# A program that ends with a 256-token tile, the last hidden part split first in front of 128-token tiles, and results handed on by block

## The chip, the cores and the metric

The kernel runs on one core of one Trainium2 chip. The metric is the device time of one execution in microseconds. TensorE (PE) multiplies, ScalarE (ACT) and VectorE (DVE) work element by element, GpSimd (POOL) issues the indirect DMAs, SyncE (SP) issues the others. Every engine works off its own queue in order and waits on semaphores.

## What is computed

Two stages follow each other: an attention of 4 x 1024 tokens over 77 context rows, added to x, and then a mixture of experts, cut here to its core:

```python
logits = jnp.einsum('bsh,he->bse', x, Wr)              # 9 experts, the best two are taken
topk_w, topk_idx = jax.lax.top_k(jax.nn.softmax(logits, axis=-1), 2)
gate = jax.nn.silu(jnp.einsum('th,ehi->tei', xf, Wg))  # 256 -> 704
hidden = gate * jnp.einsum('th,ehi->tei', xf, Wu)      # 256 -> 704
out = jnp.einsum('tei,eih,te->th', hidden, Wd, cw)     # 704 -> 256, weighted by the gate
```

The change touches only the second stage.

## The kernel before

The attention writes each token's row twice, once into the region of each of its two experts, in a DRAM table `expert_in`. The expert stage then works through 40 tiles, t = 0 to 39, listed in `TILES` (L93 to L98). A **pair** tile has two blocks of 128 tokens, a **single** tile one block. There are 3 early pairs, 29 further pairs, numbered 0 to 28, and 8 singles; `SINGLES_AFTER` (L74) names the pairs behind which a single stands. In the kernel before, the last single stands behind pair 28 and is tile 39, the last of all.

All matrices are kept as a rounded part (`hi`) and a rest (`lo`), and each product is three matmuls (`product`, L338). One tile goes through this:

- **gate and up products** (PE, `gate_up`, L1354): a pair has three units, u = 0, 1, 2, of 24, 24 and 18 matmuls of 256 columns. A single has 18 wider matmuls in one go (`single_gate_up`).
- **silu** of the gate half (ACT, `silu`), times the up half (DVE, `hidden`, gives `hid_f`), rounded by ACT (`hid_round`, gives `hid_hi`), rest by DVE (`hid_rest`, gives `hid_lo`). I call this the hidden chain; the last unit's is the "last inner part". A single's product is turned by six transposes on PE (`hid_turn`, L1448) before it is rounded.
- **down product** (PE, `down`, L1458): 34 matmuls of 256 columns for a pair (17 for each block), 17 for a single.
- **result**: ACT scales it by the gate weight (`res_move`, L1155, one ACTIVATE for each block), POOL adds it to the output in DRAM by an indirect DMA for each block (`add_results`, L927), and waits for their landing before it copies the next tile's token numbers (`note`).

While tile t is in work, the weights of tile t + 1 are split in six pieces, two at each unit of a pair: ACT rounds them (`round_pieces`, L1099, gives `wgt_hi`), DVE makes the rests (`rest_pieces`, L1932, gives `wgt_lo`). The first four pieces are the gate and up weights, which `gate_up(t + 1, 0)` waits for; the last two (1280 and 256 columns) are the down weights.

The order is written by hand. PE does the down product of a tile in the next tile's step: for a pair behind u = 1, for a single behind its gate and up products (`pair_step`, `single_step`, L1481 to L1495). At each unit of a pair step, ACT runs silu, two weight pieces, `hid_round`; DVE runs `hidden`, two rests of weights, `hid_rest`. In a single step, DVE runs the single's product, two rests, the rests of the turned tokens (`tok_rest`), two more rests, and then the single's hidden rests.

Of the kernel before, what the change touches and what calls it, by code (L numbers as in the profile page):

```python
# [70 lines left out]
EARLY_SEEN = 27  # L71
NP = 2 * B * S // W - EARLY
NS = 8
SINGLES_AFTER = (2, 6, 10, 13, 17, 21, 24, 28)  # L74
SEGS = 2 * E
assert EARLY_SEEN * 2 * P >= E * EARLY_ROWS
SPARE = 5 * W
# [27 lines left out]
def is_pair(t):  # L105
    return TILES[t][0] > 1
# [11 lines left out]
def program(nc, x, ctx_rows, fside, ln1_w, ln1_b, ln2_w, ln2_b, wq, wkv, wout, wr, wg, wu, wd, out):  # L118
# [3 lines left out]
    with ExitStack() as ctx:  # L122
# [210 lines left out]
        def turned_hid(t):  # L333

            return (unit_banks(t, 1)[:, 1, :].rearrange("p (c n) -> p c n", n=P), bank[5 - t % 2][:, KT * P:KT * P + P],
                    bank[5 - t % 2][0:FHALF, KT * P + P:KT * P + 2 * P])

        def product(to, a, b, first, last):  # L338

# [420 lines left out]
        def _(pool):  # L760
# [166 lines left out]
            def add_results(t):  # L927

                i = t % 2
                pool.wait_ge(res_ready, t + 1)  # L930
                for a in range(TILES[t][0]):
                    nc.gpsimd.indirect_dma_start(out, bass.IndirectOffsetOnAxis(ap=tok_id[i][:, a:a + 1], axis=0),  # L932
                                                 res[i][:, a, :], None, compute_op=ALU.add).then_inc(added, 16)
                pool.wait_ge(added, BLOCKS_TO[t + 1] * 16)
# [14 lines left out]
        def _(act):  # L949
# [172 lines left out]
            def silu(t, u):  # L1122

                q = (UNITS_TO[t] + u) % 2
                act.wait_ge(gu_done, UNITS_TO[t] + u + 1)
                if u < UNITS - 1:
                    nc.scalar.activation(gate_act[q][:], unit_banks(t, u)[:, :, 0:W], ACT.Silu).then_inc(silu_done, 1)
                else:
                    nc.scalar.activation(gate_act[q][:, 0, :], unit_banks(t, u)[:, 0, 0:W], ACT.Silu)
                    nc.scalar.activation(gate_act[q][FHALF:P, 1, :], unit_banks(t, u)[0:FHALF, 1, 0:W], ACT.Silu).then_inc(silu_done, 1)  # L1130
# [23 lines left out]

            def res_move(t):  # L1155
                i = t % 2
                act.wait_ge(down_done, t + 1)
                act.wait_ge(tok_noted, t + 1)
                if t > 1:
                    act.wait_ge(added, BLOCKS_TO[t - 1] * 16)  # L1160
                for a in range(TILES[t][0]):
                    ins = nc.scalar.activation(res[i][:, a, :], bank[6 + i][:, a * D:(a + 1) * D], ACT.Copy, scale=tok_gate[i][:, a:a + 1])  # L1162
                ins.then_inc(res_ready, 1)

            def pair_step(t):

                ahead = EARLY - 1 <= t < NT - 1
                src = weights_of(t + 1) if ahead else None
                for u in range(UNITS):
                    silu(t, u)  # L1170
                    if ahead:
                        round_pieces(t + 1, u, src)
                    hid_round(t, u)
                    if u == UNITS - 2 and t:
                        tok_move(t + 1)
                        if t == 2:
                            act.wait_ge(last_stored, 16)
                        res_move(t - 1)
# [30 lines left out]
        def _(pe):  # L1209
# [248 lines left out]
            def down(t):  # L1458

                i, blocks = t % 2, TILES[t][0]  # L1460
                pe.wait_ge(*down_split(t))
                pe.wait_ge(hid_ready, UNITS_TO[t + 1])
                if t > 1:
                    pe.wait_ge(res_ready, t - 1)
                elif t:
                    pe.wait_ge(tail_row_made, 1)
                    pe.wait_ge(slot_ready, T)
                else:
                    pe.wait_ge(att_added, T)
                w = [down_of(x[half_of(t)]) for x in (wgt_hi, wgt_lo)]  # L1470
                for a in range(blocks):
                    to = bank[6 + i][:, a * D:(a + 1) * D]
                    h = [x[:, :, a * P:(a + 1) * P] for x in hid[i]]
                    for f in range(FC - 1):
                        product(to, [x[:, f, :] for x in h], [x[:, f, :] for x in w], f == 0, False)

                    for x in w:
                        mm = nc.tensor.matmul(to, h[0][:, FC - 1, :], x[:, FC - 1, :], start=False, stop=x is w[1])  # L1478
                mm.then_inc(down_done, 1)

            def pair_step(t):  # L1481

                for u in range(0 if t else UNITS - 1, UNITS):
                    gate_up(t, u)
                    if u == UNITS - 2:
                        tok_turn(t + 1)
                        down(t - 1)

            def single_step(t):
# [15 lines left out]
        def _(dve):  # L1505
# [483 lines left out]
            def pair_step(t):  # L1989

                src = weights_of(t + 1) if t < NT - 1 else None
                for u in range(UNITS):
                    hidden(t, u)
                    if t < NT - 1:
                        rest_pieces(t + 1, u, src)
                    hid_rest(t, u)
                    if t < NT - 1 and u == UNITS - 2:
                        tok_rest(t + 1)

# [68 lines left out]
```

## Time and profile before

| | us |
|---|---|
| median of 3 runs | 855.67 (854.84 to 857.24) |
| the profiled execution | 854.76 |
| its span, from the first to the last instruction | 853.1 |
| PE busy | 805.5 (94% of the span) |
| DVE busy | 669.4 (78%) |
| ACT busy | 620.8 (73%) |
| POOL busy | 368.2 (43%) |
| share of PE in the chain that ended last | 84% |

The expert stage takes about the second half of the span. Rows of the timeline give, in this order: start in us, duration in us, engine, line, operation, what is written and read, and how many are merged. A bracket at the end gives the engine's idle time just before, and what ended it.

### The profile page before, as it was taken

What the parts mean: (1) busy time and instruction counts of PE and PEld (TensorE: products, weight loads), DVE (VectorE), ACT (ScalarE), POOL (GpSimd) and SP (SyncE); (2) the same over time, 40 slices, a digit from 0 to 9 for tenths busy, and PEclk for the clock granted to TensorE, in tenths of its full rate; (3) what the DMA queues carried; (4) which work ended last, traced back from release to release, by engine and by line L of the source; (5) the groups of instructions that cost most, each with busy time, mean ns of one, the idle gap of its engine ahead of it and who ended that gap; (6) DMA issues with size and microseconds to landing.
All of it is one profiled execution on the core that took longest, in us unless ns stands there. A gap on an engine that the chain in (4) does not pass through costs nothing.

```text
span 853.1 us, 19506 instructions
## 1 busy us (share of the span) xinstructions
PE 805.5 (94%) x6007; PEld 761.1 (89%) x6007; DVE 669.4 (78%) x1624; ACT 620.8 (73%) x1959; POOL 368.2 (43%) x534
## 2 busy tenths in 40 slices
PE   5999999999999999789699999999999999999993
PEld 4846899999999999789699999999999999999993
DVE  6667888889888887878578778888787888888771
ACT  4557989899889888535477777778777777777771
POOL 3020268677778766652133334233333222523232
PEclk9999999999999999879899999999999999999998
DMA  8044720310320020647547247246745565555212
GB/s 290 10 120 147 227 82 32 121 56 32 104 72 33 33 82 33 199 125 180 143 100 192 45 103 188 39 106 187 186 112 148 140 155 148 143 143 154 46 25 26
DMA packets 77675, 96.14 MB, mean 113 GB/s; under 512 B 10311, under 2 KB 64771, under 8 KB 77571
## 3 DMA queue, kind: packets, MB, share of 16 engines
q1 hardware_dynamic: 63811, 75.93, 29.4%
q0 software_dynamic: 13760, 18.96, 11.7%
q8 instruction: 48, 0.79, 0.4%
q14 instruction: 56, 0.46, 0.2%
HBM read 108.14 MB, written 31.29 MB: 163 GB/s over the span
## 4 chain that ended last, share of the span: by engine, by line
PE 84%; DMA 5%; SPq 3%; issue 2%; DVE 2%; ACT 1%; POOL 1%; DVEq 0%; POOLq 0%; ACTq 0%
PE banks L340 24%; PE banks L342 24%; PE banks L341 24%; PE banks L1327 4%; DMA valmat_dram<-val_st 2%; PE banks L1478 2%; PE banks L1341 2%; DMA expert_in<-blank 1%; SPq L596 1%; PE banks L1259 1%; PE banks L1283 1%; DMA tok<-expert_in 1%; PE banks L1295 1%; PE banks L1310 1%; DMA wkv_sb<-in_L_xattn_Wkv 0%
## 5 line engine op out<-in xcount | busy, mean ns | idle before, releaser
L340 PE MATMUL banks<-tok_t_hi,wgt_hi 128*128 128x256 f32 x704 | 202.2, 287 | 2.9 <-DVE hid_f L1947 2.5
L342 PE MATMUL banks<-tok_t_hi,wgt_lo 128*128 128x256 f32 x704 | 200.6, 285 | 0.0
L341 PE MATMUL banks<-tok_t_lo,wgt_hi 128*128 128x256 f32 x704 | 200.2, 284 | 0.0
L932 POOL DMA_INDIRECT result<-res,tok_id x72 | 117.6, 1634 | 184.5 <-ACT res L1162 154.0
L1032 ACT ACTIVATE prob<-banks,row_min 128x77 f32<-128x77 f32 x512 | 161.7, 374 | 5.7 <-DVE row_min L1674 5.7
L1939 DVE TENSOR_TENSOR wgt_lo<-wgt,wgt_hi 128x704 fp32r<-128x704 f32 x174 | 150.3, 904 | 14.7 <-ACT wgt_hi L1105 14.7
L340 PEld LDWEIGHTS banks<-tok_t_hi,wgt_hi 128*128 128x128 f32 x704 | 135.6, 193 | 5.3 <-issue 3.9
L341 PEld LDWEIGHTS banks<-tok_t_lo,wgt_hi 128*128 128x128 f32 x704 | 135.7, 193 | 0.0
L342 PEld LDWEIGHTS banks<-tok_t_hi,wgt_lo 128*128 128x128 f32 x704 | 135.6, 193 | 0.0
L1105 ACT ACTIVATE wgt_hi<-wgt 128x704 fp32r (+1 forms) x174 | 130.5, 800 | 0.5
L1032 ACT ACTIVATION_READ_ACCUMULATOR prob<-banks,row_min 128x1 f32 x512 | 130.7, 257 | 0.0
L340 PE MATMUL banks<-wgt_hi,hid_hi 128*128 128x256 f32 x360 | 105.0, 292 | 7.4 <-issue 6.1
L342 PE MATMUL banks<-wgt_hi,hid_lo 128*128 128x256 f32 x360 | 102.0, 283 | 0.0
L341 PE MATMUL banks<-wgt_lo,hid_hi 128*128 128x256 f32 x360 | 101.5, 282 | 0.0
L882 POOL TENSOR_TENSOR prob<-prob,row_inv 128x1232 f32<-128x1232 f32 x32 | 72.1, 2253 | 56.5 <-DVE row_inv L1688 56.4
L340 PE MATMUL banks<-valmat_hi,prob_t_hi 128*128 128x266 f32 x320 | 95.1, 297 | 0.7 <-DVE logits L1696 0.7
L341 PE MATMUL banks<-valmat_lo,prob_t_hi 128*128 128x266 f32 x320 | 92.3, 289 | 0.0
L342 PE MATMUL banks<-valmat_hi,prob_t_lo 128*128 128x266 f32 x320 | 92.2, 288 | 0.0
L869 POOL DMA_INDIRECT expert_in<-xn,top_slot x64 | 67.7, 1057 | 39.0 <-POOL xn L859 24.9
L340 PEld LDWEIGHTS banks<-wgt_hi,hid_hi 128*128 128x128 f32 x360 | 68.9, 191 | 9.6 <-DVE wgt_lo L1939 5.3
L921 POOL COPY tok_gate<-tok 128x2 f32<-128x2 f32 (+1 forms) x40 | 17.8, 446 | 131.0 <-DMA result<-res,tok_id 131.0
L340 PE MATMUL banks<-keymat_hi,zn_t_hi 128*128 128x462 f32 (+1 forms) x192 | 73.2, 381 | 0.0
(269 smaller groups left out, 2101.3 us busy)
## 6 DMA issues: line engine op xcount, KB each, us to landing
wgt<-in_L_ffn_Wg SPq DMA_DIRECT2D x29, 704.0 KB
wgt<-in_L_ffn_Wu SPq DMA_DIRECT2D x29, 640.0 KB
wgt<-in_L_ffn_Wd SPq DMA_DIRECT2D x29, 640.0 KB
tok<-expert_in SPq DMA_DIRECT2D x32, 258.0 KB, 2.9
spare_wgt<-in_L_ffn_Wg SPq DMA_DIRECT2D x9, 704.0 KB, 4.4
spare_wgt<-in_L_ffn_Wu SPq DMA_DIRECT2D x9, 640.0 KB, 6.6
spare_wgt<-in_L_ffn_Wd SPq DMA_DIRECT2D x9, 640.0 KB, 6.8
valmat_f<-valmat_dram SPq DMA_DIRECT2D x4, 1197.0 KB, 6.3
```

Of the source, the lines that this page charges most:

```text
L340: nc.tensor.matmul(to, a[0], b[0], start=first, stop=False)
L341: nc.tensor.matmul(to, a[0], b[1], start=False, stop=False)
L342: return nc.tensor.matmul(to, a[1], b[0], start=False, stop=last)
L869: nc.gpsimd.indirect_dma_start(expert_in, bass.IndirectOffsetOnAxis(ap=top_slot[c % 4][:, k:k + 1], axis=0), xn[c % 4][:, k, :], None).the ...
L882: nc.gpsimd.tensor_tensor(p, p, row_inv[i][:].unsqueeze(2).to_broadcast([P, H, M]), ALU.mult).then_inc(prob_ready, 1)
L921: nc.gpsimd.tensor_copy(tok_gate[i][:, 0:blocks], tok[i][:, 0:blocks, GATE])
L932: nc.gpsimd.indirect_dma_start(out, bass.IndirectOffsetOnAxis(ap=tok_id[i][:, a:a + 1], axis=0), res[i][:, a, :], None, compute_op=ALU.add ...
L1032: ins = nc.scalar.activation(prob[c % 2][:, h * M:(h + 1) * M], bank[i][:, (h - h0) * M:(h - h0 + 1) * M], ACT.Exp, bias=row_min[c % 2][:, ...
L1105: nc.scalar.activation(wgt_hi[half_of(t)][:, p0:p1], src[:, p0:p1], ACT.Copy).then_inc(weights_hi, 1)
L1327: mm = nc.tensor.transpose(bank[3 + (c * NG + g) % 2][0:n, (m - c0) * P:(m - c0 + 1) * P], prob[c % 2][:, m * P:m * P + n], ident[:])
L1341: mm = nc.tensor.transpose(turned_tokens(t)[:, k, a * P:(a + 1) * P], tok[i][:, a, k * P:(k + 1) * P], ident[:])
L1939: nc.vector.tensor_tensor(wgt_lo[i][0:rows, p0:p1], src[0:rows, p0:p1], wgt_hi[i][0:rows, p0:p1].bitcast(F32), ALU.subtract).then_inc(weig ...
```

## The change

The diff, cut to what matters:

```diff
-SINGLES_AFTER = (2, 6, 10, 13, 17, 21, 24, 28)
+SINGLES_AFTER = (2, 5, 9, 12, 16, 19, 23, 26)
+        def result_bank(t, a):
+            if t == NT - 1 and a:
+                return bank[7 - t % 2][:, 0:D]
+            return bank[6 + t % 2][:, a * D:(a + 1) * D]
@@ POOL, add_results
-                pool.wait_ge(res_ready, t + 1)
                 for a in range(TILES[t][0]):
+                    pool.wait_ge(res_ready, BLOCKS_TO[t] + a + 1)
@@ ACT, res_move
-                act.wait_ge(down_done, t + 1)
                 for a in range(TILES[t][0]):
-                    ins = nc.scalar.activation(res[i][:, a, :], bank[6 + i][:, a * D:(a + 1) * D], ...)
-                ins.then_inc(res_ready, 1)
+                    act.wait_ge(down_done, t + 1 + (a if t == NT - 1 else 0))
+                    nc.scalar.activation(res[i][:, a, :], result_bank(t, a), ...).then_inc(res_ready, 1)
@@ ACT, pair_step
                     silu(t, u)
+                    soon = u == UNITS - 1 and (t == NT - 1 or not is_pair(t + 1))
+                    if soon:
+                        hid_round(t, u)
                     if ahead:
                         round_pieces(t + 1, u, src)
-                    hid_round(t, u)
+                    if not soon:
+                        hid_round(t, u)
@@ PE, down
-                pe.wait_ge(hid_ready, UNITS_TO[t + 1])
+                pe.wait_ge(hid_ready, UNITS_TO[t + 1] - (t == NT - 1))
+                if t == NT - 1:
+                    inner(0, 0, FC - 2)
+                    pe.wait_ge(res_ready, BLOCKS_TO[t])
+                    inner(1, 0, FC - 2)
+                    pe.wait_ge(hid_ready, UNITS_TO[t + 1])
+                    for a in range(blocks):
+                        inner(a, FC - 2, FC - 1)
+                        last_inner(a).then_inc(down_done, 1)
+                    return
@@ DVE, pair_step
                     hidden(t, u)
+                    soon = u == UNITS - 1 and (t == NT - 1 or not is_pair(t + 1))
+                    if soon:
+                        hid_rest(t, u)
                     if t < NT - 1:
                         rest_pieces(t + 1, u, src)
-                    hid_rest(t, u)
+                    if not soon:
+                        hid_rest(t, u)
```

The singles now stand behind pairs 2, 5, 9, 12, 16, 19, 23 and 26, as tiles 6, 10, 15, 19, 24, 28, 33 and 37. All eight are followed by a pair. Tiles 38 and 39 are pairs 27 and 28. The number of tiles, of matmuls and of bytes is the same. At the last unit of a pair in front of a single, and of tile 39, ACT and DVE do the hidden part ahead of the weight pieces. Tile 39's down product runs its first four inner parts for both blocks, each block in a bank of its own, then the last two inner parts block by block, and signals each block. `res_ready` now counts blocks, so POOL may start on the first block of a pair when ACT has written it.

**ACT at the last unit of a pair in front of a single.** Before: silu (L1129, L1130), the single's down weights (L1105), hidden rounding (L1142, L1143), the single's silu (L1134).

```order
L1129 ACTIVATE gate_act<-banks 128x256 [waits gu_done]
L1130 ACTIVATE gate_act<-banks 64x256
L1105 ACTIVATE wgt_hi<-spare_wgt 128x1280 [waits down_done,single_d_loaded]
L1105 ACTIVATE wgt_hi<-spare_wgt 128x256
L1142 ACTIVATE hid_hi<-hid_f 128x256 [waits hid_made]
L1143 ACTIVATE hid_hi<-hid_f 64x256
...
L1134 ACTIVATE single_act<-banks 128x704 [waits gu_done]
```

The changed kernel, at the same place (its lines stand 6 further down):

```order
L1135 ACTIVATE gate_act<-banks 128x256 [waits gu_done]
L1136 ACTIVATE gate_act<-banks 64x256
L1148 ACTIVATE hid_hi<-hid_f 128x256 [waits hid_made]
L1149 ACTIVATE hid_hi<-hid_f 64x256
L1111 ACTIVATE wgt_hi<-spare_wgt 128x1280 [waits down_done,single_d_loaded]
L1111 ACTIVATE wgt_hi<-spare_wgt 128x256
...
L1140 ACTIVATE single_act<-banks 128x704 [waits gu_done]
```

The two roundings with their wait for DVE (`hid_made`) now stand ahead of the single's down weights.

**DVE at the same place.** Before: `hidden` (L1949, L1950), rests of the down weights (L1939), `hid_rest` (L1974, L1975), then the single's product.

```order
L1949 TENSOR_TENSOR hid_f<-gate_act,banks 128x256 [waits silu_done]
L1950 TENSOR_TENSOR hid_f<-gate_act,banks 64x256
L1939 TENSOR_TENSOR wgt_lo<-spare_wgt,wgt_hi 128x1280 [waits weights_hi]
L1939 TENSOR_TENSOR wgt_lo<-spare_wgt,wgt_hi 64x256 [waits weights_hi]
L1974 TENSOR_TENSOR hid_lo<-hid_f,hid_hi 128x256 [waits hid_hi]
L1975 TENSOR_TENSOR hid_hi<-hid_f,hid_hi 64x256
```

The changed kernel:

```order
L1977 TENSOR_TENSOR hid_f<-gate_act,banks 128x256 [waits silu_done]
L1978 TENSOR_TENSOR hid_f<-gate_act,banks 64x256
L2002 TENSOR_TENSOR hid_lo<-hid_f,hid_hi 128x256 [waits hid_hi]
L2003 TENSOR_TENSOR hid_hi<-hid_f,hid_hi 64x256
L1967 TENSOR_TENSOR wgt_lo<-spare_wgt,wgt_hi 128x1280 [waits weights_hi]
L1967 TENSOR_TENSOR wgt_lo<-spare_wgt,wgt_hi 64x256 [waits weights_hi]
```

The same six instructions, with `hid_rest` moved ahead of the weight rests.

**POOL at the end of the program.** Before: two scatters of tile 38 (L932), then the one of tile 39.

```order
L932 DMA result<-res,tok_id 4352x256 [waits res_ready,tok_noted]
L932 DMA result<-res,tok_id 4352x256
L932 DMA result<-res,tok_id 4352x256 [waits res_ready,tok_noted,added]
```

The changed kernel: two scatters of tile 38, two of tile 39.

```order
L938 DMA result<-res,tok_id 4352x256 [waits res_ready,tok_noted]
L938 DMA result<-res,tok_id 4352x256 [waits res_ready]
L938 DMA result<-res,tok_id 4352x256 [waits res_ready,tok_noted,added]
L938 DMA result<-res,tok_id 4352x256 [waits res_ready]
```

The last tile has one scatter more, and each scatter waits for its own block.

## Rows read from the trace of the kernel before

**Rows 1.** Windows of 20 us: us, busy us and count of each engine, PEclk, DMA.

```profile
780.00:800.00 20.00, 20.00 (x169) 19.68 (x168) 17.13 (x27) 16.62 (x31) 6.10 (x8) 1.00 0.43 101
```

**Rows 2.** Timeline of PE's weight loads, those that start behind a wait.

```profile
461.98 0.19 PEld L340 LDWEIGHTS banks<-tok_t_hi,wgt_hi 128*128 128x128 f32 x1 [0.18 <-DVE wgt_lo L1939]
...
472.49 0.19 PEld L340 LDWEIGHTS banks<-tok_t_hi,wgt_hi 128*128 128x128 f32 x1 [0.16 <-issue]
...
775.89 0.19 PEld L340 LDWEIGHTS banks<-wgt_hi,hid_hi 128*128 128x128 f32 x1 [0.80 <-DVE wgt_lo L1939]
...
780.72 0.19 PEld L340 LDWEIGHTS banks<-tok_t_hi,wgt_hi 128*128 128x128 f32 x1 [0.18 <-DVE wgt_lo L1939]
...
833.09 0.19 PEld L340 LDWEIGHTS banks<-wgt_hi,hid_hi 128*128 128x128 f32 x1 [1.28 <-DVE wgt_lo L1939]
...
840.10 0.19 PEld L340 LDWEIGHTS banks<-wgt_hi,hid_hi 128*128 128x128 f32 x1 [2.27 <-issue]
```

**Rows 3.** Timeline of PE: starts of singles' products (L340), turns of tokens (L1341).

```profile
770.93 0.40 PE L340 MATMUL banks<-wgt_hi,tok_t_hi 128*128 128x512 f32 x1
...
797.08 0.60 PE L1341 MATMUL banks<-ident,tok 128*128 128x128 f32 x4
...
821.75 0.38 PE L1341 MATMUL banks<-ident,tok 128*128 128x128 f32 x2
...
828.12 0.39 PE L340 MATMUL banks<-wgt_hi,tok_t_hi 128*128 128x512 f32 x1
```

**Rows 4.** Timeline of ACT behind the last unit of the pair before a single.

```profile
771.92 1.58 ACT L1105 ACTIVATE wgt_hi<-spare_wgt 128x1280 fp32r<-128x1280 f32 x2
...
773.41 0.40 ACT L1142 ACTIVATE hid_hi<-hid_f 128x256 fp32r<-128x256 f32 x1
...
774.02 0.74 ACT L1134 ACTIVATE single_act<-banks 128x704 f32<-128x704 f32 x1
```

**Rows 5.** Timeline of DVE, same place.

```profile
772.37 0.42 DVE L1950 TENSOR_TENSOR hid_f<-gate_act,banks 64x256 f32<-64x256 f32 x1
...
773.23 1.82 DVE L1939 TENSOR_TENSOR wgt_lo<-spare_wgt,wgt_hi 128x1280 fp32r<-128x1280 f32 x2 [0.44 <-ACT wgt_hi L1105]
...
774.98 0.41 DVE L1974 TENSOR_TENSOR hid_lo<-hid_f,hid_hi 128x256 fp32r<-128x256 f32 x1
...
775.40 0.42 DVE L1975 TENSOR_TENSOR hid_hi<-hid_f,hid_hi 64x256 fp32r<-64x256 f32 x1
...
775.85 0.42 DVE L1959 TENSOR_TENSOR single_hid<-single_act,banks 128x256 f32<-128x256 f32 x1
...
778.99 1.68 DVE L1939 TENSOR_TENSOR wgt_lo<-wgt,wgt_hi 128x704 fp32r<-128x704 f32 x2
```

**Rows 6.** Timeline of ACT and DVE in a pair behind a pair.

```profile
756.86 0.84 ACT L1162 ACTIVATE res<-banks,tok_gate 128x256 f32<-128x256 f32 x2 [0.90 <-PE banks L1478]
...
759.01 0.38 ACT L1129 ACTIVATE gate_act<-banks 128x256 f32<-128x256 f32 x1 [1.31 <-PE banks L342]
...
760.25 0.42 DVE L1950 TENSOR_TENSOR hid_f<-gate_act,banks 64x256 f32<-64x256 f32 x1
```

**Rows 7.** Timeline of ACT and POOL at the end of the program.

```profile
837.48 0.84 ACT L1162 ACTIVATE res<-banks,tok_gate 128x256 f32<-128x256 f32 x2 [5.52 <-PE banks L1478]
...
839.09 1.57 POOL L932 DMA_INDIRECT result<-res,tok_id  x1 [5.20 <-ACT res L1162]
...
840.97 1.56 POOL L932 DMA_INDIRECT result<-res,tok_id  x1 [0.30 <-issue]
...
842.40 0.47 ACT L1162 ACTIVATE res<-banks,tok_gate 128x256 f32<-128x256 f32 x1 [3.29 <-PE banks L1478]
...
845.01 1.56 POOL L932 DMA_INDIRECT result<-res,tok_id  x1 [2.48 <-DMA result<-res,tok_id]
```

**Rows 8.** Timeline of POOL: two copies of gate weights.

```profile
779.01 0.91 POOL L921 COPY tok_gate<-tok 128x1 f32<-128x1 f32 x1 [4.98 <-DMA result<-res,tok_id]
...
796.16 0.19 POOL L921 COPY tok_gate<-tok 128x2 f32<-128x2 f32 x1 [3.11 <-DMA result<-res,tok_id]
```

More of the change, by code:

```diff
@@ L1161, in res_move @@
                 for a in range(TILES[t][0]):
-                    ins = nc.scalar.activation(res[i][:, a, :], bank[6 + i][:, a * D:(a + 1) * D], ACT.Copy, scale=tok_gate[i][:, a:a + 1])
-                ins.then_inc(res_ready, 1)
+                    act.wait_ge(down_done, t + 1 + (a if t == NT - 1 else 0))
+                    nc.scalar.activation(res[i][:, a, :], result_bank(t, a), ACT.Copy, scale=tok_gate[i][:, a:a + 1]
+                                         ).then_inc(res_ready, 1)
             def pair_step(t):
@@ L1170, in pair_step @@
                     silu(t, u)
+                    soon = u == UNITS - 1 and (t == NT - 1 or not is_pair(t + 1))
+                    if soon:
+                        hid_round(t, u)
                     if ahead:
                         round_pieces(t + 1, u, src)
-                    hid_round(t, u)
+                    if not soon:
+                        hid_round(t, u)
                     if u == UNITS - 2 and t:
-                        tok_move(t + 1)
+                        if t < NT - 1:
+                            tok_move(t + 1)
                         if t == 2:
@@ L1461, in down @@
                 pe.wait_ge(*down_split(t))
-                pe.wait_ge(hid_ready, UNITS_TO[t + 1])
+                pe.wait_ge(hid_ready, UNITS_TO[t + 1] - (t == NT - 1))
                 if t > 1:
-                    pe.wait_ge(res_ready, t - 1)
+                    pe.wait_ge(res_ready, BLOCKS_TO[t - 1])
                 elif t:
@@ L1470, in down, with inner, last_inner @@
                 w = [down_of(x[half_of(t)]) for x in (wgt_hi, wgt_lo)]
-                for a in range(blocks):
[L1472 to L1478, printed above, removed]
+                to = [result_bank(t, a) for a in range(blocks)]
+                h = [[x[:, :, a * P:(a + 1) * P] for x in hid[i]] for a in range(blocks)]
+                def inner(a, f0, f1):
+                    for f in range(f0, f1):
+                        product(to[a], [x[:, f, :] for x in h[a]], [x[:, f, :] for x in w], f == 0, False)
+                def last_inner(a):
+                    for x in w:
+                        mm = nc.tensor.matmul(to[a], h[a][0][:, FC - 1, :], x[:, FC - 1, :], start=False, stop=x is w[1])
+                    return mm
+                if t == NT - 1:
[7 more added lines that the diff above has]
+                    return
+                for a in range(blocks):
+                    inner(a, 0, FC - 1)
+                    mm = last_inner(a)
                 mm.then_inc(down_done, 1)
@@ L1485, in pair_step @@
                     if u == UNITS - 2:
-                        tok_turn(t + 1)
+                        if t < NT - 1:
+                            tok_turn(t + 1)
                         down(t - 1)
```

## The prediction

> **What bounds the kernel now.** I read the page first, then the timeline of PE's waits, then ACT and DVE around each wait, and last the end of the program. In the expert stage PE runs without a pause over most of the time: from 780 to 800 us it is busy 20.00 us with 169 matmuls, 0.118 us each, at a granted clock of 1.00 [rows 1]. So the order of the tiles costs nothing in itself, and only PE's waits and the tail behind its last matmul can move. There are few. In each of the seven middle singles PE waits twice: 0.75 to 0.81 us on the weight-load queue before the down product of the pair ahead of it, and in five of them 0.17 to 0.18 us before the gate product of the pair behind it; in five, a third wait of 0.16 to 0.17 us follows at the pair after that [rows 2]. The last single costs more: 1.28 us, and 2.27 us before its own down product, the turned hidden chain being uncovered.
>
> The reader should look at what ends the first two. The first is noted as a weight rest (L1939), but those were done long before; the wait ends at 775.89, just behind the DVE instruction at 775.40 + 0.42 = 775.82, the hidden rest [rows 2, 5]. The second ends at 780.72, just behind the last weight rest, 778.99 + 1.68 = 780.67, and from 773.23 to there DVE never pauses [rows 5]. **So in a single's step DVE is the bound, not PE**: whatever PE saves at the first wait, it meets DVE's last weight rest again at the second.
>
> **The change, part by part.** *Hidden part first, in front of a single.* DVE's product ends at 772.37 + 0.42 = 772.79 [rows 5]. ACT, free since 771.9, now waits for it: it rounds at 772.82 and 773.13 (the two start 0.3 apart and end at 773.5), and takes the down weights at 772.82 + 0.61 = 773.43, where before it took them at 771.92 [rows 4]. DVE makes the hidden rests at 773.55 to 774.4. PE wants them at about 775.3 (its weight-load queue runs dry at 775.89 - 0.80 = 775.1, and what it has loaded is worked off some 0.2 later), so the first wait, 0.6 of PE's time, goes. But DVE could start the weight rests 1.31 us behind ACT's start (771.92 to 773.23); now that is 773.43 + 1.31 = 774.74. Before, it started them at 773.23 and then spent 775.85 - 774.98 = 0.87 on the hidden rests, as if it had started at 774.10. Its whole chain is 774.74 - 774.10 = 0.64 us later, and the last gate and up rest ends at 781.31 in place of 780.67. PE reaches the next gate product at 780.72 - 0.18 - 0.6 = 779.95 and waits 1.4 us there. Against before, that product starts **0.64 us later**. ACT isn't late for anything: the single's silu starts at 774.9 in place of 774.02 and is done at 775.7, where DVE wants it at 776.5. SP and POOL wait for nothing that moves here except the refill of the spare weights, which has three pairs of time.
>
> *The pair behind it.* Before, it took 472.49 - 461.98 = 10.51 us, with the third wait of 0.16 in it, for the token rests at the end of DVE's chain [rows 2]. There the delay fades: DVE did the single's hidden rests behind a gap, now without; I work out its token rests about 0.35 us late where PE comes 0.64 late, so the third wait goes. The pair takes 10.35. Each single costs 0.64 - 0.16 = **0.48 us more** than now. Bounds: 0 if DVE isn't delayed, 0.64 if the third wait stays.
>
> *The last single becomes a middle one.* From the first single to the last, before: 26 pairs and 7 singles; now 24 pairs and 7. Two steps of pairs take 821.75 - 797.08 = 24.67. The last single's gate product started at 828.12 [rows 3]; now the eighth starts at 828.12 - 24.67 + 7 x 0.48 = 806.8. Its step took 780.72 - 770.93 = 9.79, now 10.43, and the pair behind it 10.35. Tile 39 starts at 827.6.
>
> *The tail, from there (G = 827.6).* 48 matmuls are 5.7; the down product of tile 38, 34 matmuls, 4.0. ACT moves its first block from G + 9.95 to G + 10.4 (0.47) [rows 7]. POOL starts its scatter 0.77 behind the result (837.48 + 0.84 to 839.09), the second 1.88 later, and their landing let it go on at 845.01, 4.04 behind the second's start [rows 7]. That gives G + 11.2, 13.05, and free at G + 17.1. Meanwhile PE's last unit, 18 matmuls, ends at G + 11.8; silu starts at G + 12.1 (2.15 behind the result's move, 756.86 to 759.01), the product ends 1.66 later at G + 13.75 (760.67) [rows 6], rounding takes 0.75, rests 0.9: ready at G + 15.4. PE's 24 first-stage matmuls fill to G + 14.65, so it waits 0.8, against 1.28 and 2.27 before. Five matmuls, 0.9 with their drain: G + 16.35; ACT 0.47: G + 16.8; POOL starts at G + 17.6, the second scatter at G + 19.45. From the last scatter's start to the end of the span took 853.1 - 845.01 = 8.1 [rows 7]. End: G + 27.55.
>
> The price of the finer `res_ready` is nothing in the middle, where POOL waits for ACT in most tiles. In the tail the second bank and the block's own signal save one block: without them the first result would come 0.6 later. A second scatter has a wait of its own now, which had cost between 0 and, at worst, the 0.77 of an unmet wait; I take 0, since it is met long before.
>
> **The sum.** 827.6 + 27.55 = 855.15, against 853.1: **+2.05 us**. In its parts: seven middle singles +3.4, the last single and its two pairs recast, and the tail, -1.3 together. The profiled execution took 854.76, so it would be 856.8; the median of the runs shown is 0.9 above that one, and on the median the forecast is 855.67 + 2.05 = **857.7 us**, 0.24% more. A measurement here can tell about 0.3% (2.6 us) from no change, so this is "within", but near its upper edge.
>
> **The rivals.**
>
> *A, DVE not delayed.* If the hidden part went first at no cost to DVE's chain (the gap of 0.44 before the weight rests [rows 5] is the only room seen), the singles would stay at 9.79 and 10.51: 828.12 - 24.67 + 9.79 + 10.51 = 823.75, + 27.55 = 851.3, or -1.8: 853.9 us. Even here the first wait's 0.6 isn't won, since the second's time is DVE's. For it speaks only that ACT's and DVE's instructions overlap a little at their edges.
>
> *B, slower: the delay doesn't fade.* The third wait stays, because ACT's silu of the pair behind the single comes 0.64 late and DVE's chain hangs on it from there. It decides if DVE's token rests are later by more than PE's arrival, some 0.5 us. Price 8 x 0.16 = 1.3: +3.3, 859.0 us. My margin there is only 0.15 us, so this is strong. A longer landing of the last four scatters would cost about as much: 4.7 us median over all of them against 3.8 at the end.
>
> *C, POOL's copies take DVE's time.* At 779.01 a copy on POOL took 0.91 us while DVE made rests, at 796.16 one took 0.19 [rows 8]; DVE lost nothing. If in the new order the copies come first, DVE loses two of 0.19 in each single, on its bound chain: 8 x 0.38 = 3.0, 860.7 us. The Trainium skill ("SBUF — State Buffer", Who interferes with whom) says that a DVE instruction with two SBUF inputs and a GpSimd one that reads SBUF exclude each other, and that whichever issues first keeps the other waiting. By that rule, the trace's 0.91 is POOL losing; C is DVE losing.
>
> **How the numbers follow.** Forecast 0.55 (of it 0.15 over the 0.3% edge), A 0.16 (of it 0.07 below the edge), B 0.25 (0.19 above), C 0.04. Faster 0.07, within 0.3% 0.55, slower 0.38. The range goes from 854.0, which leaves out the better half of A, to 860.0, which leaves out C and the worst of B.
>
> **What would show it.** Right: no wait before the pair's down product in a single's step; a wait of 1.3 to 1.5 us on the weight-load queue before the next gate product, ended by L1967; ACT starting the single's down weights 1.5 us later; a wait of some 0.8 us before the last ten matmuls; 8.1 us from the last scatter. Wrong: if single and following pair together take 20.3 us or less (A), or 20.9 or more (B); or if the last scatter starts other than 19.5 us behind tile 39's first product.

## The result, and the profile after

| | before | after |
|---|---|---|
| median | 854.84 us (7 runs, 853.0 to 857.24) | 858.77 us (7 runs, 856.71 to 860.88) |
| ratio | 1 | 1.0050, interval 1.0030 to 1.0071 |
| profiled execution | 854.76 us, span 853.1 us | 858.77 us, span 857.2 us |
| granted clock, mean | 0.982 | 0.98 |

The changed kernel is slower, by 0.5%. The median lies in the forecast range (854.0 to 860.0), 1.1 us over the forecast of 857.7. Part of this nearness is luck: the kernel before came out 0.83 us lower than in the runs that the forecast started from (854.84 for 855.67), so the change by the medians is 3.9 us, and by the ratio 4.3, where 2.05 was forecast. And the whole interval lies at or beyond 0.3%, and the forecast had called "within 0.3%" the likeliest. So the direction and most of the mechanism were right, and the size was half of what came. In spans, in which the prediction's sum was made, it said +2.05 us, and the profiled execution shows +4.1. Where the other 2.05 us came from is worked out below.

The profile page of after. First the busy time of each engine, with its share of the span and its instructions:

```profile
PE 803.0 (94%) x6007; PEld 760.3 (89%) x6007; DVE 671.8 (78%) x1624; ACT 620.5 (72%) x1959; POOL 369.2 (43%) x534
```

Then the groups of matmuls by line and operands: busy us, mean ns of one, idle us just before them, and what ended most of that:

```profile
L346 PE MATMUL banks<-tok_t_hi,wgt_hi 128*128 128x256 f32 x704 | 202.3, 287 | 13.9 <-DVE wgt_lo L1967 11.4
...
L346 PE MATMUL banks<-wgt_hi,hid_hi 128*128 128x256 f32 x360 | 105.4, 293 | 0.9 <-DVE hid_hi L2003 0.6
```

That is the change in two rows. The down product has hardly any idle time left, 0.9 us; the gate product, reading `tok_t_hi`, has 13.9 us in front of it, and the weight rests of DVE (L1967) end 11.4 of them. Before, these two groups had 7.4 and 2.9 us. PE's waits didn't go; they moved one product further and grew.

The timeline of PE's weight loads of after, those that start behind a wait (in brackets how long, and what ended it), answers to [rows 2]:

```profile
463.08 0.19 PEld L346 LDWEIGHTS banks<-tok_t_hi,wgt_hi 128*128 128x128 f32 x1 [1.75 <-DVE wgt_lo L1967]
...
773.26 0.19 PEld L346 LDWEIGHTS banks<-tok_t_hi,wgt_hi 128*128 128x128 f32 x1 [1.64 <-DVE wgt_lo L1967]
...
818.82 0.19 PEld L346 LDWEIGHTS banks<-tok_t_hi,wgt_hi 128*128 128x128 f32 x1 [1.65 <-DVE wgt_lo L1967]
...
844.84 0.19 PEld L346 LDWEIGHTS banks<-wgt_hi,hid_hi 128*128 128x128 f32 x1 [0.77 <-DVE hid_hi L2003]
```

All eight singles have one such wait, of 1.64 to 1.75 us, in place of one of 0.75 to 0.81 in the seven middle singles and a second of 0.17 to 0.18 in five of them. At the end one wait of 0.77 us stands where there had been 1.28 and 2.27.

The timeline of DVE of after at tile 33, a single whose product starts at 762.72, answers to [rows 5]:

```profile
764.16 0.42 DVE L1978 TENSOR_TENSOR hid_f<-gate_act,banks 64x256 f32<-64x256 f32 x1
...
765.37 0.43 DVE L2002 TENSOR_TENSOR hid_lo<-hid_f,hid_hi 128x256 fp32r<-128x256 f32 x1 [0.79 <-ACT hid_hi L1149]
...
766.54 1.82 DVE L1967 TENSOR_TENSOR wgt_lo<-spare_wgt,wgt_hi 128x1280 fp32r<-128x1280 f32 x2 [0.31 <-ACT wgt_hi L1111]
768.39 0.42 DVE L1987 TENSOR_TENSOR single_hid<-single_act,banks 128x256 f32<-128x256 f32 x1
...
771.53 1.68 DVE L1967 TENSOR_TENSOR wgt_lo<-wgt,wgt_hi 128x704 fp32r<-128x704 f32 x2
```

ACT at the same place, answering to [rows 4]:

```profile
764.61 0.42 ACT L1148 ACTIVATE hid_hi<-hid_f 128x256 fp32r<-128x256 f32 x1 [0.92 <-DVE hid_f L1978]
...
765.25 1.56 ACT L1111 ACTIVATE wgt_hi<-spare_wgt 128x1280 fp32r<-128x1280 f32 x2
766.71 0.73 ACT L1140 ACTIVATE single_act<-banks 128x704 f32<-128x704 f32 x1
```

Read them against the start of the single's product. ACT now waits 0.92 us for DVE's product and takes the down weights 2.53 us behind the start (765.25 - 762.72), where before it was 0.99 (771.92 - 770.93 [rows 3, 4]). DVE stands idle for 0.79 and 0.31 us, and its last weight rest ends at 771.53 + 1.68 = 773.21, 0.05 ahead of PE's gate product. The bound is where the prediction put it.

The end of the program, POOL's scatters (with what each waited for), answers to [rows 7]:

```profile
840.66 1.56 POOL L938 DMA_INDIRECT result<-res,tok_id  x1 [7.10 <-ACT res L1168]
...
847.08 1.56 POOL L938 DMA_INDIRECT result<-res,tok_id  x1 [2.99 <-ACT res L1168]
...
848.94 1.56 POOL L938 DMA_INDIRECT result<-res,tok_id  x1 [0.30 <-issue]
```

The first of these rows is tile 38's; the other two are tile 39's, one for each block, 1.86 us apart. POOL waits for ACT's result before the first of them, and for no landing. From the start of the last to the end of the span it is 857.2 - 848.94 = 8.26 us.

### The profile page after: what moved, and what is told of

Same layout as the page of the kernel before. It is cut to its first block, busy times and chain, and to the rows that moved or that the text cites. A ratio compares the mean times of both kernels' runs of the same rounds, so it can differ in the third digit from the quotient of the medians.

```text
span 857.2 us, 19507 instructions
## 1 busy us (share of the span) xinstructions
PE 803.0 (94%) x6007; PEld 760.3 (89%) x6007; DVE 671.8 (78%) x1624; ACT 620.5 (72%) x1959; POOL 369.2 (43%) x534
## 4 chain that ended last, share of the span: by engine, by line
PE 75%; DVE 8%; DMA 5%; ACT 3%; SPq 3%; issue 3%; POOL 1%; DVEq 1%; ACTq 0%; POOLq 0%
PE banks L346 22%; PE banks L348 21%; PE banks L347 21%; PE banks L1338 4%; DVE wgt_lo L1967 4%; DMA valmat_dram<-val_st 2%; PE banks L1491 1%; PE banks L1352 1%; DMA expert_in<-blank 1%; ACT wgt_hi L1111 1%; SPq L602 1%; PE banks L1270 1%; PE banks L1306 1%; DMA tok<-expert_in 1%; DVE tok_t_lo L1951 1%
## 5 line engine op out<-in xcount | busy, mean ns | idle before, releaser
L346 PE MATMUL banks<-tok_t_hi,wgt_hi 128*128 128x256 f32 x704 | 202.3, 287 | 13.9 <-DVE wgt_lo L1967 11.4
L938 POOL DMA_INDIRECT result<-res,tok_id x72 | 121.4, 1686 | 192.3 <-ACT res L1168 170.8
L1967 DVE TENSOR_TENSOR wgt_lo<-wgt,wgt_hi 128x704 fp32r<-128x704 f32 x174 | 150.6, 907 | 12.5 <-ACT wgt_hi L1111 11.4
L1053 ACT ACTIVATE prob_t_hi<-banks 128x512 fp32r<-128x512 f32 (+1 forms) x96 | 48.8, 543 | 32.8 <-PE banks L1338 32.8
```

The costliest lines, as they stand in the source:

```text
L346: nc.tensor.matmul(to, a[0], b[0], start=first, stop=False)
L1053: ins = nc.scalar.activation(prob_t[c % 2][0][0:rows, m0:m1, :], turned_bank(c, g, rows, m0 - c0, m1 - c0), ACT.Copy)
L1967: nc.vector.tensor_tensor(wgt_lo[i][0:rows, p0:p1], src[0:rows, p0:p1], wgt_hi[i][0:rows, p0:p1].bitcast(F32), ALU.subtract).then_inc(weig ...
```

## The experiments

The theory after the result: the new order makes DVE's chain late by more than PE's first wait was worth; the new places and the two-stage end together save a little; results by block do nothing. The main rival: a single's step is not bound by DVE's chain at all, and the time came with the new places of the singles or with the way the program ends. The experiments ran in three groups, each beside the kernel before, whose medians there were 854.16 (e1 to e4), 853.3 (e5 to e8) and 853.62 us (e9, e10).

### e1: the old order in front of singles, all else as after

```diff
-                    soon = u == UNITS - 1 and (t == NT - 1 or not is_pair(t + 1))
+                    soon = u == UNITS - 1 and t == NT - 1
```

(on ACT and on DVE)

> The changed kernel with the old order in front of the eight singles (weight pieces first, then the hidden part); placement, two-stage down product and results by block stay. Theory (the hidden part first delays DVE's chain, which bounds a single's step): single and following pair together go back from 21.02 to 20.30 us, 8 x 0.72 = 5.8 us less than the changed kernel, so about 1.7 us under the kernel before (853.1 us where before takes 854.8). Rival (the placement of the singles or the tail costs the time): the time stays within 1 us of the changed kernel, 3 to 4 us over before.

Measured: 852.93 us, ratio 0.9984 (0.9971 to 0.9997). PE's weight loads around the last single:

```profile
807.33 0.19 PEld L346 LDWEIGHTS banks<-wgt_hi,hid_hi 128*128 128x128 f32 x1 [0.75 <-issue]
...
822.82 0.19 PEld L346 LDWEIGHTS banks<-tok_t_hi,wgt_hi 128*128 128x128 f32 x1 [0.26 <-issue]
...
838.40 0.19 PEld L346 LDWEIGHTS banks<-wgt_hi,hid_hi 128*128 128x128 f32 x1 [0.77 <-DVE hid_hi L2003]
```

The old waits are back, the end keeps its single wait of 0.77, and without the new order the change would be a small gain, 0.16% (1.4 us), barely clear of the noise. At the first single, single and following pair take 20.44 us (450.40 to 470.84), expected 20.30. One thing was not foreseen: the third wait, 0.16 to 0.17 us before [rows 2], is 0.23 to 0.26 in all eight places. The kernel to compare with is e3 below, which has the same places of the singles and no results by block: there the third wait is 0.16 to 0.17 us, and a short distance (between singles with two pairs between them) 44.89 to 44.97 us, where e1 has 44.95 to 45.05.

### e2: only the new order, on the kernel before

```diff
                     silu(t, u)
+                    soon = u == UNITS - 1 and not is_pair(t + 1)
+                    if soon:
+                        hid_round(t, u)
                     if ahead:
                         round_pieces(t + 1, u, src)
-                    hid_round(t, u)
+                    if not soon:
+                        hid_round(t, u)
```

(and the same with `hid_rest` on DVE)

> The kernel before with only the hidden part first in front of its eight singles. Theory: seven middle singles cost 0.72 us more each, +5.0; the last single, where no weights follow, wins its first wait of 1.0 us: together +4.0 us over before (858.8). Rival (the order wins the first wait of 0.6 us and DVE hides the rest): 7 x 0.6 + 1.0 = 5.2 us under before.

Measured: 857.51 us, ratio 1.0038 (1.0026 to 1.0051). Its weight loads, the last middle single and the last single:

```profile
787.23 0.19 PEld L340 LDWEIGHTS banks<-tok_t_hi,wgt_hi 128*128 128x128 f32 x1 [1.75 <-DVE wgt_lo L1943]
...
845.28 0.19 PEld L340 LDWEIGHTS banks<-wgt_hi,hid_hi 128*128 128x128 f32 x1 [2.27 <-issue]
```

Seven waits of 1.64 to 1.77 us, and from the first single's product to the last one's 380.39 us in place of 375.94: 4.45 us over seven singles, 0.64 each. The last single gives about 1.0 us back, as expected, since its first wait is gone (from its first product to the end of the span it is 23.97 us, before 24.98). **The new order alone makes the loss**, with the old places and the old end; the rival falls. Short and long distances between singles are 45.50 to 45.53 and 57.84 to 57.91 us, the same as in after (45.50 to 45.58, 57.83 to 57.91), so with this order the results by block cost nothing.

### e3: only the new places, on the kernel before

```diff
-SINGLES_AFTER = (2, 6, 10, 13, 17, 21, 24, 28)
+SINGLES_AFTER = (2, 5, 9, 12, 16, 19, 23, 26)
```

(and no move and turn of tokens behind the last tile, which is now a pair)

> The kernel before with only the new places of the singles, so that it ends with a pair whose down product runs whole, in one bank, behind the last hidden rest. Theory: up to tile 39 as in e1; from there the 34 matmuls (4.0 us and 0.3 of drain) start at G + 15.4, both results move by G + 20.6, the last scatter starts at G + 23.3 and the span ends at G + 31.4 where the changed kernel needs 27.9: 3.5 us over e1, about 1.8 us over before (856.6). Rival (the new end is worth its gain by itself, without the stages): at or under before.

Measured: 858.43 us, ratio 1.0047 (1.0035 to 1.0059), 2 us more than expected. The last pair's down product, whole and in one bank, waits for the whole hidden part of both blocks:

```profile
840.78 0.19 PEld L340 LDWEIGHTS banks<-wgt_hi,hid_hi 128*128 128x128 f32 x1 [3.62 <-issue]
```

Behind this wait, a window (us, busy us and count of PE, PEld, DVE, ACT and POOL, then the granted clock, the DMA share and GB/s):

```profile
840.80:846.60 5.80, 5.78 (x34) 5.59 (x34) 0.00 (x0) 0.00 (x0) 0.00 (x0) 0.71 0.21 23
```

From the start of the first of the 34 matmuls to that of the last it is 5.49 us (840.82 to 846.31), where at a granted clock of 1.00 it would be 33 x 0.118 = 3.9: this is 1.6 of the missing 2 us. So the new places alone are a loss, 0.47%; they are no gain without the two-stage end.

### e8: e1 with the whole down product in one bank at the end

```diff
-            if t == NT - 1 and a:
+            if False:
                 return bank[7 - t % 2][:, 0:D]
...
-                if t == NT - 1:
-                    inner(0, 0, FC - 2)
-                    pe.wait_ge(res_ready, BLOCKS_TO[t])
-                    inner(1, 0, FC - 2)
-                    pe.wait_ge(hid_ready, UNITS_TO[t + 1])
-                    for a in range(blocks):
-                        inner(a, FC - 2, FC - 1)
-                        last_inner(a).then_inc(down_done, 1)
-                    return
```

(and the two counts of signals that belong to it)

> As e1 (old order in front of the singles, new places, results by block), but tile 39's down product runs whole and in one bank behind the last hidden rest. Theory: PE waits some 3.6 us for the last hidden rest, and then has 34 matmuls to do in place of 10, part of them at a granted clock under 1: 5 us over e1, about 858 us, and within 0.5 us of the kernel with the new places alone, since handing on by block starts only tile 39's first scatter 0.4 us earlier. Rival (handing on by block is what shortens the tail): within 2 us of e1.

Measured: 857.04 us, ratio 1.0052 (1.0032 to 1.0073): 5.8 us over e1 by the ratios (0.0068 of 854), 4.1 by the medians. The same wait as in e3 stands in its timeline:

```profile
837.16 0.29 PEld L346 LDWEIGHTS banks<-wgt_hi,hid_hi 128*128 128x128 f32 x1 [3.61 <-issue]
```

And the window behind it (columns as in e3), with the same fall of the clock:

```profile
837.20:843.00 5.80, 5.80 (x27) 5.80 (x28) 0.00 (x0) 0.00 (x0) 0.00 (x0) 0.50 0.14 19
```

From tile 39's first product to the end of the span it takes 33.8 us, in e1 27.9. So the two stages and banks are worth 5.8 to 5.9 us. In this trace the clock makes 2.8 of them: the 34 matmuls start over 6.69 us (837.19 to 843.88), for 3.9 at 1.00. This is the good part of the change. Results by block, which e8 keeps, don't show as a gain in the time: 0.52% over before, in e3 without them 0.47%. In the traces they start the first of the last two scatters 1.26 us behind ACT's result (844.28 to 845.54), in e3 1.62 (846.63 to 848.25), the 0.4 us that was expected.

### e4: after, with DVE's longest weight rest cut short

This kernel leaves out part of the computation: of the first down piece of a single, DVE makes the rests of 256 columns rather than 1280.

```diff
                     dve.wait_ge(weights_hi, pieces_to(t) + n + 1)
+                    if n == 2 * KT and not is_pair(t):
+                        p1 = p0 + D
```

> The changed kernel, but DVE makes the rests of only 256 of the 1280 columns of a single's first down piece: this leaves out part of the weights' rests, 1.07 us of DVE's chain in each single. Theory (DVE bounds the step): the wait before the next pair's gate product falls from 1.38 us of PE's time to 0.3, 8 x 1.07 = 8.6 us less than the changed kernel, about 850.2 us. Rival (the wait hangs on ACT's later start or on PE itself): less than 2 us of gain.

Measured: 850.33 us, ratio 0.9947 (0.9933 to 0.9961). PE's weight loads at tile 33, the first of two views:

```profile
766.89 0.19 PEld L346 LDWEIGHTS banks<-tok_t_hi,wgt_hi 128*128 128x128 f32 x1 [0.74 <-DVE wgt_lo L1969]
```

DVE's product for the same single, the second view:

```profile
762.01 0.42 DVE L1989 TENSOR_TENSOR single_hid<-single_act,banks 128x256 f32<-128x256 f32 x1 [0.20 <-ACT single_act L1140]
```

Work taken from DVE comes off the time, one engine away from the one that is 94% busy: the seven distances from the first single to the last sum to 350.13 us, in after to 355.74, 0.80 per single. DVE's chain is the bound there. Eight times 0.80 is 6.4 us, not the expected 8.6; that the median still meets the expected 850.2 is in part luck: in the traces the first single starts 0.76 us earlier than in after (451.77 and 452.53), which the edit doesn't touch, and each kernel's runs are spread over 3 to 4 us. The waits were expected at 0.3 and stay at 0.74 to 0.86 (one is 1.22): DVE now reaches the single's product before ACT's silu is done and waits 0.20, and part of what the short rest saves goes there.

### e5 and e6: the single's down pieces in its own step

In the order of the kernel, ACT and DVE split a single's down weights in the pair's last unit, in front of everything that the next gate product needs. In e5 (from after) and e6 (from before) they split them in the single's own step, behind the next pair's gate and up pieces. Of the diff its core; the rest counts the pieces in the new order.

```diff
-                    if t < NT - 1:
+                    if t < NT - 1 and (u < UNITS - 1 or is_pair(t + 1)):
                         rest_pieces(t + 1, u, src)
...
                     rest_pieces(t + 1, 1, src)
+                rest_pieces(t, UNITS - 1, spare_wgt[:])
                 single_hid_rest(t)
```

(on DVE; on ACT the same with `round_pieces`)

> The changed kernel, but a single's down weights (pieces 5 and 6) are rounded by ACT and their rests made by DVE in the single's own step, behind the next pair's gate and up weights, where both engines idle. Theory (DVE's chain up to the next gate product is the bound): 1.75 us leave it, single and following pair take about 19.7 us in place of 21.02, 8 x 1.3 = 10.5 us less than the changed kernel, about 847.5 us. Rival (the moved rests are late for the pair's own step, whose chain from silu to the token rests sets 10.5 us): half of that, about 852 to 853 us.

Measured, e5: 848.09 us, ratio 0.9929 (0.9911 to 0.9948). At the first single, single and following pair take 19.76 us (450.47 to 470.23), as the theory had it.

> The kernel before with only that move of the singles' down weights. Theory: single and following pair take 19.7 in place of 20.3 us, 7 x 0.64 = 4.5 us, and the last single loses its first wait of 1.0 us: 5 to 5.5 us under before, about 849 us. Rival (DVE is late for the pair): 1 to 2 us under before.

Measured, e6: 848.32 us, ratio 0.9947 (0.9928 to 0.9966). The wait in the single's step is gone in both; what is left stands at the tile behind the pair, 0.27 to 0.55 us, and in e6 two waits for tokens of 0.32 and 0.60. In e5's profiled execution (851.08 us, the upper end of its runs) new waits of 0.79 to 2.65 us stand before three turns of tokens, here on the weight-load queue:

```profile
714.63 0.71 PEld L1360 LDWEIGHTS banks<-ident,tok 128*128 128x128 f32 x4 [2.65 <-DMA tok<-expert_in]
```

POOL's timeline ahead of it:

```profile
708.89 1.54 POOL L934 COPY tok_gate<-tok 128x1 f32<-128x1 f32 x1 [8.64 <-DMA result<-res,tok_id]
```

POOL notes the gate weights and ids of tile t + 2 only behind the landing of tile t's results, and the buffer of the tokens becomes free for the next load behind that. Here POOL stood idle for 8.64 us until the landing, and in part of this time (700 to 705 us) the DMA engines were 97% busy. Behind PE's wait of 2.65 us the granted clock fell (columns as in e3):

```profile
714.63:719.00 4.37, 4.37 (x25) 4.37 (x26) 2.37 (x4) 0.83 (x3) 0.32 (x1) 0.62 0.91 237
```

### e9 and e10: POOL copies the ids before it waits for the landing

```diff
+                if t + 2 < NT:
+                    note(t + 2)
                 pool.wait_ge(added, BLOCKS_TO[t + 1] * 16)
...
-                if t + 2 < NT:
-                    note(t + 2)
```

(with a third buffer for gate weights and ids; e9 is e5 with it, e10 is after with it)

> e5, and POOL copies the token numbers and gate weights of tile t + 2 behind the issue of tile t's scatters and ahead of the wait for their landing, into a third pair of small buffers, so that the tokens' load no longer hangs on that landing. Theory (in e5 PE's waits before turning tokens, 1.30, 0.79 and 2.65 us, come from POOL's copies being held behind slow landings, up to 8.6 us): these waits go, 4 us under e5, some 10 us under before. Rival (the loads themselves are slow under the weights' traffic): within 1 us of e5.

Measured, e9: 847.37 us, ratio 0.9933 (0.9919 to 0.9948).

> The changed kernel with only that earlier copy on POOL. Both theories: PE never waits for tokens there behind tile 3, so nothing is won in the singles; within 1 us of the changed kernel, 3 to 5 us over before. If POOL's copies now keep DVE waiting (they read the same memory as its weight rests), it is slower than the changed kernel by up to 3 us.

Measured, e10: 857.68 us, ratio 1.0060 (1.0038 to 1.0082). In e9's trace the waits for tokens are gone, and from the first single to the last it takes 346.56 us where e5's trace has 351.39; but its ratio is that of e5, so the expected 4 us missed. The runs of e5 lie between 845.7 and 851.1, those of e9 between 845.7 and 849.0. The waits for tokens may stand in some of e5's executions and not in others; one trace of each can't tell, and this stays open. In e10 nothing changed, the waits of 1.64 to 1.75 included, as expected.

### e7: the new order on ACT alone

DVE keeps the old order in front of singles, ACT has the new one: of after, the one line `soon = ...` of DVE goes back to the form in e1.

> The changed kernel with ACT's new order but DVE's old one in front of the singles, so that DVE waits for the late weight pieces first and makes the hidden rests behind them. Theory: DVE's chain starts its weight rests at the same late time and has the hidden rests (0.87 us) behind them: 8 x 0.87 = 7 us over the changed kernel, about 865 us, with PE's wait back before the pair's down product (1.8 to 2.1 us). Rival (the delay comes from the number of hand-overs, not from DVE's chain): within 2 us of the changed kernel.

Measured: 870.12 us, ratio 1.0197 (1.0175 to 1.0219), 5 more than expected. In DVE's timeline it comes to the weight rests first and waits for ACT's late rounding, with the hidden rests queued behind it:

```profile
712.84 1.82 DVE L1967 TENSOR_TENSOR wgt_lo<-spare_wgt,wgt_hi 128x1280 fp32r<-128x1280 f32 x2 [1.96 <-ACT wgt_hi L1111]
```

PE's weight loads behind it:

```profile
715.49 0.27 PEld L346 LDWEIGHTS banks<-wgt_hi,hid_hi 128*128 128x128 f32 x1 [2.31 <-DVE wgt_lo L1967]
```

PE waits 2.26 to 2.32 us in all eight places. Behind four of them the granted clock fell, behind four it did not. Windows that begin with the wait's end, of one that fell, one that didn't, and another that fell (columns as above):

```profile
503.30:507.50 4.20, 4.20 (x23) 4.20 (x24) 4.20 (x8) 1.41 (x3) 1.16 (x2) 0.59 0.03 8
...
669.00:673.10 4.10, 4.05 (x34) 4.08 (x35) 4.10 (x8) 1.48 (x3) 1.22 (x2) 1.00 0.04 8
...
715.50:719.60 4.10, 4.08 (x21) 4.10 (x22) 4.10 (x8) 1.45 (x3) 1.07 (x2) 0.58 0.31 68
```

At 1.00, 34 or 35 matmuls start in 4.1 us; behind the fall, 21 to 23. Against after, a distance between singles grew by 1.0 us without the fall (expected 0.87) and by some 2.5 with it. That is the part that the expectation lacked.

## Why the prediction was right or wrong

**In a single's step DVE is the bound.** Right, and the step on which the sign hangs. e2 shows it with the order alone, e4 by taking work from DVE, e5 and e6 by taking it out of the way.

**DVE's chain is 0.64 us late.** Right in kind, too small. The forecast put the start of the weight rests 3.81 us behind the single's product (774.74 - 770.93), and it is 3.82 (766.54 - 762.72). The next step failed: how long until DVE is at the single's product behind them. Before, DVE's instruction behind that rest started 1.75 us after it (773.23 to 774.98 [rows 5]), though the rest lasts 1.82; the sum kept this overlap. In after the next starts 1.85 us after it (766.54 to 768.39), with no overlap. The sum subtracted the hidden rests with the seam behind them (775.40 to 775.85, 0.45 for a rest of 0.42) and kept the overlap in front of them. What now stands behind the weight rest is the single's product. Two causes that suggest themselves are not it. The silu that the product waits for was done 0.95 us before (766.71 + 0.73 = 767.44). And the load from the table of tiles into a register (L1958), which names the weights of the pair's slot and stands in the queue between the two, ends at 767.43; in the kernel before the same load stands between these two rows, and the overlap is there, 1.74 us for 1.82:

```profile
783.13 1.82 DVE L1939 TENSOR_TENSOR wgt_lo<-wgt,wgt_hi 128x1280 fp32r<-128x1280 f32 x2 [0.39 <-ACT wgt_hi L1105]
784.87 0.67 DVE L1947 TENSOR_TENSOR hid_f<-gate_act,banks 128x512 f32<-128x512 f32 x1
```

What the seams in the last parts of these traces have in common is where an operand starts. The second halves of the product and of the hidden rest, which read or write from partition 64 on, start with no overlap too (0.44 behind a product of 0.42, 763.72 to 764.16 in after; 0.42 behind a rest of 0.41, 774.98 to 775.40 before). The single's product reads a bank from partition 0, where the last read of a bank (L1978) had begun at partition 64. In both kernels it starts with no overlap, only that before it stood behind a short rest. This fits, but no run tried it by itself. The gate product starts 10.55 us behind the single's product, where it was 9.80 (452.53 to 463.08, and 452.18 to 461.98 before): 0.75 in place of 0.64.

**The pair behind gives back 0.16.** Nearly right. From that gate product to the next tile it took 10.54 us before and 10.42 in after (463.08 to 473.50), and in after no weight load there stands behind a wait. PE's matmuls of after at that seam, at tile 33's pair:

```profile
783.59 0.28 PE L348 MATMUL banks<-tok_t_hi,wgt_lo 128*128 128x256 f32 x1
783.74 0.36 PE L346 MATMUL banks<-tok_t_hi,wgt_hi 128*128 128x256 f32 x1
```

Two matmuls 0.15 us apart at the seam, where it was 0.25 to 0.28 before. So the third wait cost PE 0.10 to 0.14, some 0.12, not the 0.16 that stands on the weight-load queue; the first wait likewise is 0.80 there and 0.60 in PE's own rows. So a single costs 0.75 - 0.12 = 0.63, by the distances 0.64 in e2, and 0.61 in after against e3, which has the same places; forecast 0.48.

**Rival B** said that the third wait stays and gave +3.3 us. The time came out near it, and the prediction's own test (single and pair together 20.9 us or more) pointed to it, with 20.97 us at the first single and 21.02 at tile 33. But its mechanism didn't happen: the third wait is gone. The test was too coarse, since it could not tell a larger delay from a smaller give-back; only the two steps apart can. There are also two kinds of places: before, the two steps together take 20.33 to 20.34 us at five singles and 20.40 to 20.41 at the second and the fifth. The forecast's 20.30 was made up from two places of the lower kind, while the last single of after is of the other.

**Rival A** falls: its 0.44 us of room before the weight rests is a gap of 0.31 in after. **Rival C** falls too. POOL's second copy met DVE's rest head on. DVE of after:

```profile
769.33 1.68 DVE L1967 TENSOR_TENSOR wgt_lo<-wgt,wgt_hi 128x704 fp32r<-128x704 f32 x2
```

And POOL:

```profile
769.36 0.90 POOL L928 CAST tok_id<-tok 128x1 int32<-128x1 f32 x1
```

DVE, first by 0.03 us, took its 1.68 as in the undisturbed row at 771.53; POOL took 0.90, where the same cast takes 0.19 elsewhere (780.16 us). From the single's product to the end of the last weight rest DVE needs 4.82 us in after (768.39 to 773.21) and 4.82 before (775.85 to 780.67), and all eight gate products start 10.54 to 10.55 us behind their single's, so POOL cost DVE nothing at any of them. The Trainium skill ("SBUF — State Buffer", Who interferes with whom) says that whichever of the two issues first keeps the other waiting; the trace agrees for the order in which DVE is first. The other order, which C needed, came up here only at an edge: POOL's first copy (769.23, 0.19 us) began 0.10 us ahead of DVE's rest, which still lasted 1.68.

**The last single, the tail.** Tile 39's first product starts at 829.29, forecast 827.6. Tile 39's first scatter starts 17.79 us behind that (847.08), forecast 17.6; the second 19.65, forecast 19.45; the end of the span 27.91, forecast 27.55. PE's wait of 0.77 was forecast at 0.8. So the tail was right to 0.36 us: half lies before the last scatter, half in its landing, 8.26 us in place of 8.1.

**Results by block cost nothing.** Right for the kernel as changed (e2 and after have the same distances), wrong as a general statement: with the old order the third wait grows by 0.06 to 0.10 us (e1 and e8 against e3), and seven distances by 0.5 (351.97 in e1, 351.44 in e3). ACT now has a wait and a signal for each block; that these are the cost is argued and wasn't tried by itself.

**The sum.** The span came out 857.2 - 855.15 = 2.05 us over the forecast:

| part | forecast | measured | miss |
|---|---|---|---|
| start of the first single's product | 452.18 (as before) | 452.53 | 0.35 |
| seven distances to the eighth single | 354.6 | 355.74 | 1.1 |
| last single and the pair behind it | 20.78 | 21.02 | 0.24 |
| tail | 27.55 | 27.91 | 0.36 |

Of the 1.1, 7 x (0.61 - 0.48) = 0.9 is the order: 0.11 a single from DVE's seam, the rest from the third wait's true price. The other 0.2 comes with the new places: e3, which has them without the order, needs 351.44 us, the kernel before less two pairs 375.94 - 24.67 = 351.27. Three of e3's seven singles are at places of the longer kind, before two, which explains 0.07 of it. The first line isn't the change's: that start lies between 449.2 and 454.1 in kernels that do not differ up to there. Such a spread of the earlier stage is as large as the whole effect, which is why the distances inside the expert stage were used to judge, not the spans.

**The chances.** Forecast +2.05 us with 0.15 above the 0.3% edge, and B above it. The measured ratio is 0.5%. A term that is paid eight times was wrong by 0.15 on 0.48, and eight times this, 1.2 us, is enough to cross the edge at 2.6. The chance for "slower" of 0.38 was too low for a forecast so near to it.

## What to carry to other kernels

Before an instruction is put forward to end a wait, follow the engine that makes it to its next delivery: if that engine has no gap before the bottleneck's next need, the wait moves and grows by what the reordering costs. The wait to look at is the second, and the piece that could go behind both (here the single's down weights, needed last and split first) is worth more: e5 and e6 came out 0.7% and 0.5% under the kernel before. A cost that repeats should be taken between two starts on the bottleneck engine itself, at every kind of place, since the wait on a queue that runs ahead of it is larger than what it costs (0.80 us on the weight-load queue here, 0.60 in the matmuls).

## What the runs showed of the hardware that was not expected

A wait on TensorE can cost its clock. Behind the waits of up to 1.75 us in after the granted clock stayed at 1.00 in all eight places, one of which (columns as above) is

```profile
773.30:776.30 3.00, 3.00 (x25) 3.00 (x26) 2.82 (x5) 1.15 (x2) 2.70 (x2) 1.00 0.80 223
```

Behind eight waits of 2.26 to 2.32 us in e7 it fell in four. The wait of 2.27 us before the last single's down product is the same in three traces: behind it the clock stayed in the kernel before [rows 2] and in e6, and fell in e2. The kernel before, then e2:

```profile
840.10:842.40 2.30, 2.24 (x17) 2.06 (x17) 0.00 (x0) 0.00 (x0) 2.00 (x2) 1.00 0.51 57
```

```profile
845.28:847.60 2.32, 2.29 (x12) 2.32 (x13) 0.00 (x0) 0.00 (x0) 2.02 (x2) 0.61 0.51 56
```

Behind the wait of 2.65 us in e5 it fell, and behind those of 3.6 us in e3 and e8 both times. The lower level, 1.2 GHz in place of 2.4, shows as 27 matmuls in 5.8 us in e8, 0.21 us each, against 0.118 [rows 1]. A fall cost about 1.5 us in e7, 1.6 in e3 and 2.8 in e8. In e2 it made the last 17 matmuls 1.2 us longer (3.17 us from the first start to the last, before 1.96), but the end came only 0.2 us later, since the last scatter waits for a landing in any case. So, as an estimate, a wait that grows from 1.7 to 2.3 us may cost three to four times its growth (0.6 + 1.5 us for 0.6), in some places and not in others; what decides between them these runs don't show.
